# A kernel's first loads: half of x asked for later, half behind the first weight block, and 13 warm-up matmuls in place of 18

## Chip, cores and metric

The kernel runs on one core of one Trainium2 chip. The metric is the device time of one execution in microseconds (us). The time before is the median of three executions.

## What is computed

For each of 8 batches, an index picks one of 8 weight matrices. The batch's rows x (256 x 1024) are multiplied by it, giving y. y then goes through a 1024 x 1024 projection `W_up` plus the low-rank correction of the one expert (of 4) whose gate logit is largest. x is added at the end.

```python
y = jnp.einsum('bsi,boi->bso', x, weight[adapter_ids])
logits = y_flat @ gate_w.T + expert_bias
one_hot = jax.nn.one_hot(jnp.argmax(logits, axis=-1), E)
base_out = jnp.einsum('bth,oh->bto', y, W_up)
z = jnp.einsum('nh,erh->ner', y_flat, lora_A)
delta = jnp.einsum('neh,ne->nh', jnp.einsum('ner,ehr->neh', z, lora_B), one_hot)
out = x + base_out + delta
```

Everything is float32 in and out.

## The kernel before

**Arithmetic.** To keep float32 accuracy on TensorE (PE), each operand is split in two: a high part, which ScalarE (ACT) makes by casting to the matmul's format (`x_hi`, `first_w_hi`, `w_hi_part`), and a low part, which VectorE (DVE) makes by subtracting the high part from the original (`x_lo`, `first_w_lo`, `w_lo_part`). Each product is then several matmuls. For y it is two for each chunk of 128 inputs: L745 with the high weights on both parts of x (512 columns), and L747 with the low weights on the high part of x (256 columns).

**Staging.** For each batch, `first_product` makes y in 8 blocks of 128 outputs. Block n needs one 512 KB piece of weights, called W0, W1, ... here. Each block is 8 pairs of L745 and L747, one pair for each chunk k. The x of a batch (1 MB) comes in two halves of 512 KB: chunks 0 to 3 are the first half, chunks 4 to 7 the second. ACT and DVE split x in four quarters of two chunks, and W0 in four quarters as well; later weight blocks are split in halves. `block_done` counts finished blocks, and ACT then copies a part of the result (`small`, L361) which DVE adds up (L533). After the 8 blocks come the projection, the gates and the correction, then the next batch.

**Order of the work at the start.** All orders are written out by hand. The queue of SyncE (SP) first reads the batch's matrix index from memory into a register. That takes two loads, both at L212: one of the address of `ids`, one of the index itself. Only then can it issue the DMA of W0 (L221), then W1, W2, W3, and from there pieces of `W_up` (L232) and W4 to W6 in turn. ACT's queue issues the two halves of the first x at once (L453), since they depend on no index. DVE meanwhile clears a tile (L706), casts it (L708), and PE runs `WARM` matmuls on these zeros (L730), whose results nobody uses. PE takes its instructions in order, so the first true matmul can't start before the last of these.

The first true matmul (L745 of block 0, k = 0) waits for the first quarter of x and the first of W0, both split. PE then waits again at k = 2, 4 and 6 for the next quarters of each:

```python
if n == 0 and k % QK == 0:
    pe.wait_ge(w_ready, k // QK + 1)
if c == 0 and k % XK == 0:
    pe.wait_ge(x_ready, b * XQ + k // XK + 1)
```

Of the kernel before, what the change touches and what calls it, by code (L numbers as in the profile page):

```python
# [25 lines left out]
def build(nc, xT, x, ids, w, w_up, gl, lora_b, bias, out):  # L26
    B, S, H = x.shape
    KC = H // P
# [16 lines left out]
    XQ = 4  # L45
    XK = KC // XQ
    XD = 2
    XS = KC // XD
# [2 lines left out]
    PARTS = 7  # L51
    SUMS = 5
    STEPS = 9
    WARM = 18
    BLOCKS = B * OC
    assert T == 2 and 4 * ER == P and HALF == 512 and B >= 4 and 2 * GL <= P

# [18 lines left out]
    with ExitStack() as ctx:  # L76
# [22 lines left out]
        x_raw = nc.alloc_sbuf_tensor_at("x_raw", [P, 2, KC, S], F32, offset=x_at)  # L99
# [39 lines left out]
        def sem(name):  # L139
            return ctx.enter_context(nc.semaphore(name))  # L140

        x_raw_in = [sem(f"x_raw_in{d}") for d in range(XD)]
# [7 lines left out]
        warm_step = sem("warm_step")  # L150
# [59 lines left out]
        def _(sp):  # L210
            def adapter(b):
                i = sp.value_load(ids[0:1, b:b + 1])  # L212
                i = i + (i < 0) * A
                i = i * (i > -1)
                i = i + (i > A - 1) * (A - 1 - i)
                return sp.snap(i, min_val=0, max_val=A - 1)

            def load_w(n, i):
                if n >= RAWS:
                    sp.wait_ge(block_done, n - RAWS + 1)  # L220
                sp.dma_start(w_raw[:, n % RAWS, :], w[bass.ds(i * OC + n % OC, 1), :, :].rearrange("a p n -> (a p) n")  # L221
                             ).then_inc(w_raw_in[n % RAWS], 16)
# [40 lines left out]
            def load_blocks(first, stop, i):  # L263
                for n in range(first, min(stop, BLOCKS)):
                    if n % OC == 0:
                        i = adapter(n // OC)
                    load_w(n, i)
                return i

            i = adapter(0)  # L270
            i = load_blocks(0, 4, i)
            for n in range(4, OC):
                load_unit(n - 4)
                i = load_blocks(n, n + 1, i)
# [6 lines left out]
            i = load_blocks(OC, OC + RAWS - 1, i)  # L281
            load_x(1)
            i = load_blocks(OC + RAWS - 1, OC + RAWS, i)
# [4 lines left out]
            for b in range(1, B):  # L288
# [5 lines left out]
                i = load_blocks(first, first + 3, i)  # L294
                load_rows(b)
                i = load_blocks(first + 3, first + OC - 1, i)
                if b + 1 < B:
                    load_x(b + 1)
                i = load_blocks(first + OC - 1, first + OC, i)
# [29 lines left out]
        def _(act):  # L329
            def x_hi(b, q):  # L330
                act.wait_ge(x_raw_in[q * XD // XQ], (b + 1) * 16)
                ks = slice(q * XK, (q + 1) * XK)
                act.copy(x_hilo[:, 0, ks, :], x_raw[:, 1, ks, :]).then_inc(x_hi_ready, 1)  # L333

            def first_w_hi(q):
                act.wait_ge(w_raw_in[0], 16)
                part = slice(q * QK * P, (q + 1) * QK * P)
                act.copy(w_hi[:, 0, part], w_raw[:, 0, part]).then_inc(w_hi_ready, 1)
# [109 lines left out]
                for n in splits_after(b):  # L448
                    w_hi_part(n)

            for d in range(XD):
                ks = slice(d * XS, (d + 1) * XS)
                act.dma_start(x_raw[:, 1, ks, :], xT[0, :, ks, :]).then_inc(x_raw_in[d], 16)  # L453
            for q in range(XQ - 1):
                x_hi(0, q)
            for q in range(QUARTERS // 2):
                first_w_hi(q)
            x_hi(0, XQ - 1)
            for q in range(QUARTERS // 2, QUARTERS):
                first_w_hi(q)  # L460
            for n in range(1, AHEAD):
                w_hi_part(n)
# [8 lines left out]
        def _(dve):  # L471
            def x_lo(b, q):
                dve.wait_ge(x_hi_ready, b * XQ + q + 1)
                ks = slice(q * XK, (q + 1) * XK)
                dve.tensor_tensor(x_hilo[:, 1, ks, :], x_raw[:, 1, ks, :], x_hilo[:, 0, ks, :].bitcast(F32),  # L475
                                  ALU.subtract).then_inc(x_ready, 1)

            def first_w_lo(q):
                dve.wait_ge(w_hi_ready, q + 1)
                part = slice(q * QK * P, (q + 1) * QK * P)  # L480
                dve.tensor_tensor(w_lo[:, 0, part], w_raw[:, 0, part], w_hi[:, 0, part].bitcast(F32),  # L481
                                  ALU.subtract).then_inc(w_ready, 1)
# [223 lines left out]
            dve.memset(warm_f[:, :], 0.0).then_inc(warm_step, 1)  # L706
            dve.wait_ge(warm_step, 1)
            dve.tensor_copy(warm[:, :], warm_f[:, :]).then_inc(warm_ready, 1)  # L708
            for q in range(XQ - 1):
                x_lo(0, q)  # L710
            for q in range(QUARTERS // 2):
                first_w_lo(q)
            x_lo(0, XQ - 1)
            for q in range(QUARTERS // 2, QUARTERS):
                first_w_lo(q)
            for n in range(1, AHEAD):
                w_lo_part(n)
# [8 lines left out]
        def _(pe):  # L726
            def warm_up():
                pe.wait_ge(warm_ready, 1)
                for _ in range(WARM):
                    pe.matmul(ps_y[0][:, :], warm[:, 0:P], warm[:, :], start=True, stop=True)  # L730
# [177 lines left out]
```

## Time and profile before

| | |
|---|---|
| median of 3 runs | 386.61 us (386.48 to 386.88) |
| the profiled execution, own time | 386.45 us |
| its span, first to last instruction | 384.4 us |
| PE busy | 375.4 us (98%) |
| DVE busy | 263.5 us (69%) |
| ACT busy | 163.0 us (42%) |

All positions below are microseconds from the start of the span. The profiled execution is 2.05 us longer than its span, and 0.16 us below the median. A busy share tells how much an engine worked over the whole span; what the change can move lies in the first 12 us, and must be read there.

### The profile page before, as it was taken

Reading aid. Unit: us, or ns where it says so; the run is one execution under the profiler, and the core shown is the slowest. Engines: PE = TensorE matmul, PEld = TensorE weight load, DVE = VectorE, ACT = ScalarE, POOL = GpSimd, SP = SyncE. Lnnn points to the kernel's source line nnn. Section 1 sums busy time; section 2 is a strip of 40 time slices with the busy share of each in tenths; the row PEclk is TensorE's granted clock in tenths of the full one; section 3 lists DMA queues with packets and bytes.
Section 4 is the critical chain, followed back from the end, with each engine's and each line's share of the span. In section 5 each row is a group of like instructions: output and inputs, shape, how many; then the busy total and the mean of one; then the engine's idle time right before and its main releaser. Section 6 shows DMA issues by size and latency. Waiting matters only on the chain.

```text
span 384.4 us, 5419 instructions
## 1 busy us (share of the span) xinstructions
PE 375.4 (98%) x1946; PEld 317.2 (83%) x1946; DVE 263.5 (69%) x501; ACT 163.0 (42%) x329; POOL 4.7 (1%) x15
## 2 busy tenths in 40 slices
PE   6999999999999999999999999999999999999996
PEld 5888888888888788887888878888888878888885
DVE  4878766787658997579636795477864788446743
ACT  5658524554146623565114642255412554044300
POOL 1000200000000000000000000000000000000000
PEclk9999999999999999999999999999999999999999
DMA  7999946860089600875037640476304861160002
GB/s 240 413 378 353 410 192 220 319 226 2 0 309 333 233 2 14 287 271 195 2 122 247 234 163 2 165 282 202 119 0 175 318 218 59 49 226 0 2 0 109
DMA packets 19081, 68.12 MB, mean 177 GB/s; under 512 B 2288, under 2 KB 2416, under 8 KB 19056
## 3 DMA queue, kind: packets, MB, share of 16 engines
q1 hardware_dynamic: 18768, 66.74, 48.4%
q10 hardware_dynamic: 288, 1.05, 0.8%
q8 instruction: 15, 0.25, 0.3%
q14 instruction: 10, 0.08, 0.1%
HBM read 59.39 MB, written 8.39 MB: 176 GB/s over the span
## 4 chain that ended last, share of the span: by engine, by line
PE 83%; DMA 5%; DVE 3%; issue 3%; ACT 2%; SPq 1%; POOLq 1%; POOL 0%; DVEq 0%
PE ps_y L745 26%; PE ps_y L747 13%; PE ps_u L752 6%; PE ps_u L754 5%; PE ps_u L756 5%; DMA gl_raw<-gl_dram 4%; PE ps_g L765 4%; PE ps_v L752 4%; PE ps_v L756 4%; PE ps_v L754 4%; PE ps_p L752 2%; PE ps_p L754 2%; PE ps_p L756 2%; DVE w_lo L488 2%; ACT w_hi L346 1%
## 5 line engine op out<-in xcount | busy, mean ns | idle before, releaser
L745 PE MATMUL ps_y<-x_hilo,w_hi 128*128 128x512 f32 x512 | 181.0, 398 | 1.4 <-DVE w_lo L481 1.1
L747 PE MATMUL ps_y<-x_hilo,w_lo 128*128 128x256 f32 x512 | 143.7, 281 | 0.0
L745 PEld LDWEIGHTS ps_y<-x_hilo,w_hi 128*128 128x128 f32 x512 | 96.1, 188 | 25.6 <-DVE w_lo L481 1.5
L747 PEld LDWEIGHTS ps_y<-x_hilo,w_lo 128*128 128x128 f32 x512 | 96.7, 189 | 0.3
L488 DVE TENSOR_TENSOR w_lo<-w_raw,w_hi 128x512 fp32r<-128x512 f32 x126 | 81.2, 687 | 16.7 <-ACT w_hi L346 15.7
L361 ACT COPY small<-ps_y 128x256 f32<-128x256 f32 x64 | 23.8, 372 | 116.4 <-PE ps_y L747 116.4
L346 ACT CAST w_hi<-w_raw 128x512 fp32r<-128x512 f32 x126 | 71.8, 623 | 0.7 <-DMA w_raw<-w_dram 0.7
L533 DVE TENSOR_TENSOR y_raw<-ps_y,small 128x256 f32<-128x256 f32 x64 | 27.1, 423 | 52.4 <-ACT small L361 52.3
L752 PE MATMUL ps_u<-up_hi,y_parts 128*128 128x512 f32 x112 | 44.6, 398 | 0.0
L754 PE MATMUL ps_u<-up_lo,y_parts 128*128 128x512 f32 x112 | 43.8, 391 | 0.0
L756 PE MATMUL ps_u<-up_hi,y_parts 128*128 128x512 f32 x112 | 43.7, 390 | 0.0
L364 ACT CAST y_parts<-y_raw 128x512 fp32r<-128x512 f32 x50 | 28.8, 619 | 11.4 <-DVE y_raw L539 11.4
L544 DVE TENSOR_TENSOR y_parts<-y_raw,y_parts 128x512 fp32r<-128x512 f32 x50 | 32.5, 685 | 1.3 <-ACT y_parts L364 0.9
L752 PE MATMUL ps_v<-up_hi,y_parts 128*128 128x512 f32 x64 | 25.9, 404 | 2.3 <-DVE y_parts L544 2.3
L551 DVE TENSOR_TENSOR rows<-ps_u,rows 128x512 f32<-128x512 f32 x26 | 17.9, 687 | 13.9 <-PE ps_u L756 13.9
L756 PE MATMUL ps_v<-up_hi,y_parts 128*128 128x512 f32 x64 | 25.1, 392 | 0.0
L754 PE MATMUL ps_v<-up_lo,y_parts 128*128 128x512 f32 x64 | 25.0, 391 | 0.0
L756 PEld LDWEIGHTS ps_u<-up_hi,y_parts 128*128 128x128 f32 x112 | 21.0, 188 | 4.6
L752 PEld LDWEIGHTS ps_u<-up_hi,y_parts 128*128 128x128 f32 x112 | 21.1, 188 | 4.4 <-DVE up_lo L495 0.2
L754 PEld LDWEIGHTS ps_u<-up_lo,y_parts 128*128 128x128 f32 x112 | 21.0, 188 | 3.8
L475 DVE TENSOR_TENSOR x_hilo<-x_raw,x_hilo 128x512 fp32r<-128x512 f32 x32 | 20.5, 686 | 4.2 <-ACT x_hilo L333 3.5
L378 ACT CAST zT<-ps_y 128x128 fp32r<-128x128 f32 x16 | 3.5, 269 | 41.1 <-PE ps_y L784 41.1
(81 smaller groups left out, 355.5 us busy)
## 6 DMA issues: line engine op xcount, KB each, us to landing
w_raw<-w_dram SPq DMA_DIRECT2D x64, 512.0 KB, 4.4
rows<-x_dram SPq DMA_DIRECT2D x16, 512.0 KB, 5.8
out_dram<-rows SPq DMA_DIRECT2D x15, 512.0 KB, 2.6
x_raw<-xT_dram SPq DMA_DIRECT2D x14, 512.0 KB, 5.0
up_raw<-w_up_dram SPq DMA_DIRECT2D x8, 512.0 KB, 11.6
up_stage<-w_up_dram SPq DMA_DIRECT2D x8, 512.0 KB, 13.9
x_raw<-xT_dram ACTq DMA_DIRECT2D x2, 512.0 KB, 4.3
lb_raw<-lora_b_dram SPq DMA_DIRECT2D x4, 128.0 KB, 13.9
```

What stands on the lines that cost most here:

```text
L346: act.copy(w_hi[:, n % RING, part], w_raw[:, n % RAWS, part]).then_inc(w_hi_ready, QUARTERS // HALVES)
L361: act.copy(small[:, c % 2, :], ps_y[c % 2][:, S:2 * S]).then_inc(y_small_ready, 1)
L364: act.copy(y_parts[:, p, :, 0, :], y_raw[:, p, :, 1, :]).then_inc(y_hi_ready, 1)
L475: dve.tensor_tensor(x_hilo[:, 1, ks, :], x_raw[:, 1, ks, :], x_hilo[:, 0, ks, :].bitcast(F32), ALU.subtract).then_inc(x_ready, 1)
L488: dve.tensor_tensor(w_lo[:, n % RAWS, part], w_raw[:, n % RAWS, part], w_hi[:, n % RING, part].bitcast(F32), ALU.subtract).then_inc(w_read ...
L533: dve.tensor_tensor(y_raw[:, p:p + 2, c % Q, 1, :], ps_y[c % 2][:, 0:S].rearrange("p (t n) -> p t n", t=T), small[:, c % 2, :].rearrange(" ...
L544: dve.tensor_tensor(y_parts[:, p, :, 1, :], y_raw[:, p, :, 1, :], y_parts[:, p, :, 0, :].bitcast(F32), ALU.subtract).then_inc(y_ready, 1)
L745: pe.matmul(ps_y[c % 2][:, :], w_hi[:, n % RING, cols], x_hilo[:, :, k, :], start=(k == 0), stop=False)
L747: last = pe.matmul(ps_y[c % 2][:, S:2 * S], w_lo[:, n % RAWS, cols], x_hilo[:, 0, k, :], start=False, stop=(k == KC - 1))
L752: pe.matmul(ps[:, :], y_parts[:, p, k, 0, :], up_hi[:, q, k, :], start=start, stop=False, skip_group_check=True)
L754: pe.matmul(ps[:, :], y_parts[:, p, k, 0, :], up_lo[:, q, k, :], start=False, stop=False, skip_group_check=True)
L756: return pe.matmul(ps[:, :], y_parts[:, p, k, 1, :], up_hi[:, q, k, :], start=False, stop=stop, skip_group_check=True)
```

## The change

Four edits, all in the start of the first batch:

- the number of matmuls on zeros is 13 instead of 18
- ACT waits for the end of DVE's first memset (`warm_step`) and then issues the DMA of the first half of x only
- SP issues the DMA of the second half of x, right behind that of W0 and ahead of that of W1
- ACT and DVE take the splits in another order: x quarters 0 and 1, W0 quarters 0 and 1, then x quarter 2, W0 quarter 2, x quarter 3, W0 quarter 3. Before it was x quarters 0, 1 and 2, W0 quarters 0 and 1, x quarter 3, W0 quarters 2 and 3

```diff
-    WARM = 18
+    WARM = 13
...
             i = adapter(0)
-            i = load_blocks(0, 4, i)
+            i = load_blocks(0, 1, i)
+            sp.dma_start(x_raw[:, 1, XS:KC, :], xT[0, :, XS:KC, :]).then_inc(x_raw_in[1], 16)
+            i = load_blocks(1, 4, i)
...
-            for d in range(XD):
-                ks = slice(d * XS, (d + 1) * XS)
-                act.dma_start(x_raw[:, 1, ks, :], xT[0, :, ks, :]).then_inc(x_raw_in[d], 16)
-            for q in range(XQ - 1):
+            act.wait_ge(warm_step, 1)
+            act.dma_start(x_raw[:, 1, 0:XS, :], xT[0, :, 0:XS, :]).then_inc(x_raw_in[0], 16)
+            for q in range(XQ // XD):
                 x_hi(0, q)
             for q in range(QUARTERS // 2):
                 first_w_hi(q)
-            x_hi(0, XQ - 1)
             for q in range(QUARTERS // 2, QUARTERS):
+                x_hi(0, q)
                 first_w_hi(q)
...
-            for q in range(XQ - 1):
+            for q in range(XQ // XD):
                 x_lo(0, q)
             for q in range(QUARTERS // 2):
                 first_w_lo(q)
-            x_lo(0, XQ - 1)
             for q in range(QUARTERS // 2, QUARTERS):
+                x_lo(0, q)
                 first_w_lo(q)
```

How the instructions stand on ACT from its first one, before (`x_raw_in0` and `x_raw_in1` count the two halves of x, `w_raw_in0` is W0's arrival):

```order
L453 DMA x_raw_52<-xT_dram 128x1024 x2
L333 ACT_TABLE_LOAD
L333 CAST x_hilo_53<-x_raw_52 128x512 [waits x_raw_in0] x2
L333 CAST x_hilo_53<-x_raw_52 128x512 [waits x_raw_in1]
L338 CAST w_hi_51<-w_raw_49 128x256 [waits w_raw_in0] x2
L333 CAST x_hilo_53<-x_raw_52 128x512 [waits x_raw_in1]
L338 CAST w_hi_51<-w_raw_49 128x256 [waits w_raw_in0] x2
L346 CAST w_hi_51<-w_raw_49 128x512 [waits w_raw_in1]
```

and on ACT of the changed kernel, where the lines stand two or three higher:

```order
L456 DMA x_raw_52<-xT_dram 128x1024 [waits warm_step]
L335 ACT_TABLE_LOAD
L335 CAST x_hilo_53<-x_raw_52 128x512 [waits x_raw_in0] x2
L340 CAST w_hi_51<-w_raw_49 128x256 [waits w_raw_in0] x2
L335 CAST x_hilo_53<-x_raw_52 128x512 [waits x_raw_in1]
L340 CAST w_hi_51<-w_raw_49 128x256 [waits w_raw_in0]
L335 CAST x_hilo_53<-x_raw_52 128x512 [waits x_raw_in1]
L340 CAST w_hi_51<-w_raw_49 128x256 [waits w_raw_in0]
L348 CAST w_hi_51<-w_raw_49 128x512 [waits w_raw_in1]
```

One DMA has left ACT, the other now waits, and both casts of the second half of x stand behind the first two of W0. DVE's subtractions have moved in the same way. On SP, from its first instructions, the piece of the difference is:

```order
 L221 ISA x2
 L221 DMA w_raw_49<-w_dram 128x1024
+L272 DMA x_raw_52<-xT_dram 128x1024
 L221 ISA
 L221 DMA w_raw_49<-w_dram 128x1024
```

The second half of x has come in between W0 and W1; every later DMA of SP's stands one place further back.

## Rows read from the trace of the kernel before

**Rows 1.** The page's engines, and PE's longest wait for a split.

```profile
PE 375.4 (98%) x1946; PEld 317.2 (83%) x1946; DVE 263.5 (69%) x501; ACT 163.0 (42%) x329; POOL 4.7 (1%) x15
...
PE ps_y L745 <- DVE w_lo L481: 1.1, 1, 1.1
```

**Rows 2.** Chain that ended last, 0 to 14 us: start us, us, what.

```profile
0.73 0.86 SPq L212
...
1.62 2.19 SPq L212
...
4.47 3.36 DMA w_raw<-w_dram
...
7.85 0.41 ACT w_hi L338
...
8.77 0.50 PE ps_y L745
...
11.73 0.13 PE ps_y L747
```

**Rows 3.** The index loads: whole run (x8), then the second batch's; ns min/median/max.

```profile
L212 SPq TENSOR_LOAD <-ids_dram_ptr x8: 862/1870/3115, 0.7 to 293.1; - x8
L212 SPq TENSOR_LOAD <-ids_dram x8: 467/551/2186, 1.6 to 295.1; - x8
...
L212 SPq TENSOR_LOAD <-ids_dram x1: 1222/1222/1222, 20.7 to 20.7; - x1
```

**Rows 4.** Timeline, 0 to 9 us: start us, us, engine line operation.

```profile
0.74 0.86 ACTq L453 DMA_DIRECT2D x_raw<-xT_dram  x2
...
0.92 0.48 DVE L706 MEMSET warm_f<- 128x512 f32 x1 [0.92 <-PEq L901]
...
1.92 5.74 PE L730 MATMUL ps_y<-warm 128*128 128x512 f32 x18 [1.92 <-DVE warm L708]
...
4.70 1.83 ACT L333 CAST x_hilo<-x_raw 128x512 fp32r<-128x512 f32 x3 [1.78 <-DMA x_raw<-xT_dram]
5.35 1.90 DVE L475 TENSOR_TENSOR x_hilo<-x_raw,x_hilo 128x512 fp32r<-128x512 f32 x3 [3.48 <-ACT x_hilo L333]
...
8.29 0.76 DVE L481 TENSOR_TENSOR w_lo<-w_raw,w_hi 128x256 fp32r<-128x256 f32 x2 [1.03 <-ACT w_hi L338]
```

**Rows 5.** Tile x_raw, 0 to 14 us: its two DMAs, issue to landing.

```profile
DMA to landing us min/median/max: 3.9/4.3/4.7
```

**Rows 6.** Timeline, 9 to 15.3 us.

```profile
9.89 1.15 ACT L346 CAST w_hi<-w_raw 128x512 fp32r<-128x512 f32 x2 [0.20 <-DMA w_raw<-w_dram]
...
10.62 2.73 DVE L488 TENSOR_TENSOR w_lo<-w_raw,w_hi 128x512 fp32r<-128x512 f32 x4
...
11.00 0.39 PE L745 MATMUL ps_y<-x_hilo,w_hi 128*128 128x512 f32 x1
...
11.34 1.14 ACT L346 CAST w_hi<-w_raw 128x512 fp32r<-128x512 f32 x2 [0.30 <-DMA w_raw<-w_dram]
...
11.69 0.39 PE L745 MATMUL ps_y<-x_hilo,w_hi 128*128 128x512 f32 x1
...
15.20 1.14 ACT L346 CAST w_hi<-w_raw 128x512 fp32r<-128x512 f32 x2 [0.16 <-DMA w_raw<-w_dram]
```

**Rows 7.** Windows of 0.5 us: busy of each engine, granted clock, DMA share, GB/s.

```profile
7.00:7.50 0.50, 0.50 (x3) 0.20 (x2) 0.26 (x1) 0.00 (x0) 0.00 (x0) 1.00 1.05 426
...
9.00:9.50 0.50, 0.50 (x4) 0.40 (x4) 0.43 (x2) 0.50 (x3) 0.00 (x0) 1.00 0.60 156
```

**Rows 8.** Matmuls on zeros, 0 to 5 us, then 5.3 to 8 us.

```profile
L730 PE MATMUL ps_y<-warm x8: 393/628/794, 1.9 to 5.0; 128*128 128x512 f32 x8
...
L730 PE MATMUL ps_y<-warm x11: 388/389/398, 5.0 to 7.3; 128*128 128x512 f32 x11
```

**Rows 9.** Timelines of ACT and POOL, from 30 us.

```profile
31.30 0.37 ACT L361 COPY small<-ps_y 128x256 f32<-128x256 f32 x1 [1.45 <-PE ps_y L747]
...
38.94 2.80 POOL L325 TENSOR_TENSOR gl_parts<-gl_raw,gl_parts 128x432 fp32r<-128x432 f32 x1 [7.01 <-ACT gl_parts L382]
```

## Prediction

> **What bounds the kernel now.** I read the page first. PE is busy for 375.4 of 384.4 us [rows 1], so what happens before PE's first true matmul is nearly all that can be won outside PE's own work, and any shift of the first block moves everything behind it. Next I read the chain that ended last, over its first 12 us, because it says what the first true matmul waited for [rows 2]. SP loads the address of the indices (0.73 to 1.59), then the index (1.62 to 3.81), computes W0's address and issues W0's DMA at 4.47. That lands 3.36 us later, at 7.83. ACT's cast and DVE's subtraction take it to PE's start at 8.77, and block 0 is done at 11.73 + 0.13 = 11.86 (the chain's last piece of it). From here I use "block 0 done" as the mark: 11.86 before.
>
> Then the timeline of the same stretch [rows 4]. The first half of x is asked for at 0.74 and ACT starts on it at 4.70, after 3.96 us. Three of its four casts run from 4.70 to 6.53 without a pause, so the second half of x was there by 5.92. The times to landing agree: 3.9 us for the first half; 4.7 us for the second, which was issued some 0.43 us after the first, hence about 1.17 + 4.7 = 5.87 [rows 4, 5]. So x is early by 2 us, and W0 is late. The matmuls on zeros end at 1.92 + 5.74 = 7.66, another 1.1 us before PE's start, and PE's wait row says so too [rows 1, 4].
>
> **Later memset, one DMA alone.** The odd row in the chain is the index load: 2.19 us [rows 2]. The same load takes a median of 0.55 us and at least 0.47 in the eight batches, and 1.22 in the second one. The load of the address takes 0.86 at the start, when nothing moves, and a median of 1.87 in the run, where transfers are mostly in flight [rows 3]. In the first batch the index load runs beside the start of x's transfers, which were asked for at 0.74. The change asks for x when the memset ends, 0.92 + 0.48 = 1.40; with the hand-over I take 1.45, later by 0.71. If x's bytes are that much later too, an index load of the quiet kind, 1.62 + 0.86 = 2.48, is over as they begin. I take 0.86, the one load of the trace that ran in silence; the bounds are 0.47 and the full 2.19. W0's issue then moves from 4.47 by 2.19 - 0.86 = 1.33 to 3.14.
>
> The Trainium skill, "DMA: Bandwidth & Descriptors", section "Latency and other measured facts", says the memory's latency is about 0.2 us on average but 2 us at high load. By that rule the shortening is real and the sum stays as it is; the spread between 0.47 and 3.1 us in the rows agrees with it [rows 3].
>
> **When W0 lands.** Two bounds. By itself W0 needs 3.36 us from issue: 3.14 + 3.36 = 6.50. But it comes behind the first half of x, and two transfers of 512 KB that start from silence landed 5.87 - 0.74 = 5.13 us after the first was asked for [rows 4, 5]: 1.45 + 5.13 = 6.58. The later one holds: 6.58, against 7.83. The first half of x lands at 1.45 + 3.96 = 5.41. Its two casts end at about 6.6 and its two subtractions at about 7.4 (each pair at the pace of 0.61 us, the first subtraction 0.65 us behind the first cast, as in rows 4). W0's first subtraction begins at about 7.3 and PE starts 0.48 us after that begins (8.29 to 8.77): near 7.8.
>
> **When the second half of x lands.** It now follows W0 on SP's queue. One transfer of 512 KB takes 1.29 us in the steady stream: W2 landed at about 11.32, W4 at about 15.18, with W3 and one piece of W_up between, so three transfers in 3.86 us [rows 6]. 6.58 + 1.29 = 7.87; before it was 5.87. This is the price of the change: what was idle-time work on ACT and DVE is now on the path. Behind a landing at L: cast of x quarter 2, its subtraction 0.65 later, W0 quarter 2 another 0.61 later, x quarter 3 another 0.36 (0.34 is the pace of the small subtractions [rows 4], and the cast of quarter 3 must be done), W0 quarter 3 another 0.61: it begins at L + 2.23. PE starts on k = 6 0.48 later, L + 2.71. Before, k = 6 started at 11.00 and the block was done at 11.86 [rows 2, 6], so done is L + 2.71 + 0.86 = L + 3.57 = 11.44. The direct way, PE's start at 7.8 + 3.09 (8.77 to 11.86), would be 10.9, so the second half of x decides, with short waits of PE at k = 4 and k = 6. Net: 11.44 - 11.86 = **-0.42 us**.
>
> **W1.** It too moves back one place on SP's queue, but up by W0's 1.25 us. It lands 1.29 behind the second half of x, at 9.16, or, if the hole in the stream that stands there now is kept (W1 was at 9.87, 2.04 behind W0, with 156 GB/s at 9.00:9.50 against 426 in the stream [rows 6, 7]), at 9.91. From landing to PE: the subtraction starts 10.62 - 9.87 = 0.75 behind, and takes 0.69 (2.73 us for four, overlapped by some hundredths, [rows 6]): 9.91 + 1.48 = 11.39 for block 1's first matmul, which stood at 11.69. So this path gives -0.30 at the latest. I take **-0.4 us** between the two. Block 2's and block 3's weights come when they came before (the stream carries the same bytes and starts 0.7 later, but has no gap between x and W0), and are needed 5 us after they land from W3 on.
>
> **The 13 matmuls.** Five fewer. Late in the stretch they are 0.23 us apart, (7.3 - 5.0) / 10 [rows 8], so the last ends near 7.66 - 1.15 = 6.5. With 18 they would end at 7.66, just under PE's new start of 7.8: this edit is worth nothing as long as the second half of x decides. It costs nothing unless the clock falls (below).
>
> **What is behind.** No later wait takes the gain back: POOL's subtraction at 38.94, which PE's gates wait for, is released by ACT, and ACT has worked without a pause since 31.30, when PE's block 7 released it [rows 9]; all of that moves with PE. Sum: 386.61 - 0.4 = **386.2 us**; the profiled one 386.45 would be 386.05, with a span of 384.0.
>
> **Rivals.**
> 1. The second half of x comes late in its new place. If the hole of 0.75 us falls on it and not on W1, it lands at 8.62 and block 0 is done at 12.19: +0.33, 386.9. The hole follows W0 in the profile, which speaks for it; that it may belong to W1's or W2's bytes speaks against.
> 2. The index load doesn't get shorter; it was slow because it was the first. W0 is issued at 4.47 and lands at 7.83 as now, the second half of x at 9.12, block 0 is done at 12.69: **+0.83 us, 387.4, slower**. It decides from the point where L + 3.57 passes 11.86: L = 8.29, W0 at 7.00, thus W0's issue at 3.64 and an index load of 1.36 us. For it: no load of the index happened in silence. Against it: the address load, just as cold, took 0.86.
> 3. The load is halfway, 1.22 as in the second batch [rows 3]: issue 3.50, W0 at 6.86, x at 8.15, done 11.72: -0.14, 386.5. The Trainium skill, "Runtime: NRT & Kernel Launch", section "The ~15µs preamble/postamble breakdown", gives 1.3 us for such a load as one trip to memory, without regard to traffic; that would nearly be this case, but the 0.47 and 0.86 of the rows speak against a fixed price.
> 4. More than forecast. One transfer alone may ramp faster than two did: W0 needed 2.3 us from where x's bytes stopped (about 5.5) to its landing. If x's first half ramps likewise and W0 follows without a gap, W0 lands near 6.2 and the second half of x at 7.5: -0.8, 385.8. PE's start bounds it at 10.9 - 11.86 = -1.0.
> 5. PE's clock. The matmuls on zeros took 628 ns at first and 389 from 5.0 us on, with starts 0.43 and 0.23 us apart [rows 8]: the lower level (1.2 GHz) until PE had worked for some 3 us, the upper one (2.4 GHz) after it, although the profile's clock column reads 1.00 throughout. The idle time ahead of PE's start grows from 1.1 to 1.3 us, with two short waits behind it. Should the clock fall, 3 us of work at half rate cost +1.5: 387.7. The 1.1 us before did not bring it down, so I give this little.
>
> **How the numbers follow.** Chances: the forecast 0.37, case 3 0.11, case 1 0.12, case 2 0.14, case 4 0.22, case 5 0.04. Faster or slower by 0.2% is 0.77 us, about what a measurement of this kernel can tell. Some three quarters of case 4 and a little of the forecast are faster by that much: 0.20. Cases 2 and 5, not quite all, are slower: 0.16. The same: 0.64. The range reaches from case 4 (385.7) to case 2 (387.4), widened a little for what I may have left out: 385.6 to 387.5.
>
> **What would show it.** In the changed kernel's chain the second L212 piece should be near 0.9 us and W0's DMA should start near 3.1 and land near 6.6. PE's first true matmul should stand near 7.8, with a wait of about 0.4 us ahead of k = 4 and 0.3 ahead of k = 6, and block 0 done near 11.4. PE's matmuls behind block 1 should be the same, all shifted. The prediction is wrong if the index load stays at 2 us, if the second half of x lands after 8.3, or if later waits of PE are new.

## Result and the profile after

The changed kernel takes 388.75 us (median of 20 runs, 387.45 to 391.68), the kernel before 386.65 (20 runs, 386.17 to 387.20): ratio 1.0054, 95% interval 1.0039 to 1.0068. It is slower by 2.1 us, where 0.4 us faster was forecast. The changed kernel's runs also spread over 4 us, those of before over 1.

The profiled execution took 387.59 us, with a span of 385.7, so it is one of the faster ones: 1.3 us more than the span before. Its chain that ended last, from the start (start us, us, what), answers to [rows 2]:

```profile
0.73 0.85 SPq L212
...
1.61 0.46 SPq L212
...
2.74 0.39 SPq L221
...
3.18 6.26 DMA x_raw<-xT_dram
...
9.46 0.63 ACT x_hilo L335
...
10.11 0.69 DVE x_hilo L478
...
11.20 0.50 PE ps_y L748
...
12.98 0.13 PE ps_y L750
```

The index load fell from 2.19 to 0.46 us, and W0's DMA starts at 2.74 instead of 4.47. But the chain no longer runs through W0. It runs through the second half of x, asked for at 3.18 and landed 6.26 us later, at 9.44. Block 0 is done at 12.98 + 0.13 = 13.11; before it was 11.86. These +1.25 us are the whole difference of the two spans. The timeline of the same stretch answers to [rows 4]:

```profile
1.44 0.38 ACTq L456 DMA_DIRECT2D x_raw<-xT_dram  x1
...
1.92 5.05 PE L733 MATMUL ps_y<-warm 128*128 128x512 f32 x13 [1.92 <-DVE warm L711]
...
5.22 1.14 ACT L335 CAST x_hilo<-x_raw 128x512 fp32r<-128x512 f32 x2 [2.09 <-DMA x_raw<-xT_dram]
...
7.34 0.71 ACT L340 CAST w_hi<-w_raw 128x256 fp32r<-128x256 f32 x2 [0.98 <-DMA w_raw<-w_dram]
...
8.26 0.50 PE L748 MATMUL ps_y<-x_hilo,w_hi 128*128 128x512 f32 x1 [1.28 <-DVE w_lo L484]
...
9.46 0.62 ACT L335 CAST x_hilo<-x_raw 128x512 fp32r<-128x512 f32 x1 [1.41 <-DMA x_raw<-xT_dram]
...
11.20 0.50 PE L748 MATMUL ps_y<-x_hilo,w_hi 128*128 128x512 f32 x1 [1.26 <-DVE w_lo L484]
```

W0 landed at 7.32, 4.58 us after its issue against 3.36 before. PE starts at 8.26, half a microsecond earlier than before, works for four chunks and then waits 1.26 us. The second half of x came 2.12 us behind W0, not 1.29. PE's waits over the whole run answer to the row of waits in [rows 1]:

```profile
PE ps_y L748 <- DVE w_lo L484: 2.5, 2, 1.3
PE ps_v L755 <- DVE y_parts L547: 2.3, 4, 0.6
```

One wait of 1.1 us has become two that sum to 2.5; the rest is as it was. The stream of bytes is where the time went; windows of 0.5 us (the last two numbers are the share of the DMA engines and GB/s):

```profile
4.50:5.00 0.50, 0.50 (x2) 0.39 (x2) 0.00 (x0) 0.00 (x0) 0.00 (x0) 1.00 0.60 139
...
6.00:6.50 0.50, 0.50 (x4) 0.41 (x3) 0.50 (x2) 0.36 (x1) 0.00 (x0) 1.00 1.05 418
...
7.00:7.50 0.50, 0.00 (x0) 0.00 (x0) 0.17 (x1) 0.16 (x1) 0.00 (x0) 1.00 0.90 221
7.50:8.00 0.50, 0.00 (x0) 0.00 (x0) 0.22 (x1) 0.50 (x2) 0.00 (x0) 1.00 1.02 287
```

There are two holes, one between the first half of x and W0, one while the second half of x is under way; in the second the engines are busy (0.90 and 1.02) but move only 221 to 287 GB/s. The kernel before had its own hole, behind W0 [rows 7], but nothing that PE needed stood in it.

Each load counts sixteen completions on its semaphore, and has landed with the last. For the second half of x the trace has the first of them at 7.72, the twelfth at 8.80 and the last at 9.44: some parts of the load come long after the others.

### The profile page after: what moved, and what is told of

It reads as the page before. It is cut to its first block, busy times and chain, and to the rows that moved or that the text cites. A ratio compares the mean times of both kernels' runs of the same rounds, so it can differ in the third digit from the quotient of the medians.

```text
span 385.7 us, 5409 instructions
## 1 busy us (share of the span) xinstructions
PE 375.2 (97%) x1941; PEld 316.3 (82%) x1941; DVE 263.3 (68%) x501; ACT 162.8 (42%) x329; POOL 4.7 (1%) x15
## 3 DMA queue, kind: packets, MB, share of 16 engines
HBM read 59.39 MB, written 8.39 MB: 176 GB/s over the span
## 4 chain that ended last, share of the span: by engine, by line
PE 83%; DMA 6%; DVE 3%; issue 3%; ACT 2%; SPq 1%; POOLq 1%; POOL 0%; DVEq 0%
PE ps_y L748 26%; PE ps_y L750 13%; PE ps_u L755 6%; PE ps_u L757 5%; PE ps_u L759 5%; DMA gl_raw<-gl_dram 4%; PE ps_g L768 4%; PE ps_v L755 4%; PE ps_v L759 4%; PE ps_v L757 3%; PE ps_p L755 2%; PE ps_p L757 2%; PE ps_p L759 2%; DMA x_raw<-xT_dram 2%; DVE w_lo L491 1%
```

## Experiments

Each kernel was timed beside the kernel before on the same chip: the median of before was 386.60 us beside experiments 1 to 4, 386.49 beside 5 to 8 and 386.56 beside 9 to 15. With each run comes its span and its mean granted clock. "Low clock" below means a mean of 0.996 or less; none of the 94 runs of the kernel before beside these experiments was below 0.998.

**1. The late asking alone.**

```diff
+            act.wait_ge(warm_step, 1)
             for d in range(XD):
                 ks = slice(d * XS, (d + 1) * XS)
                 act.dma_start(x_raw[:, 1, ks, :], xT[0, :, ks, :]).then_inc(x_raw_in[d], 16)
```

> The kernel before with one edit: ACT waits for the first memset and then asks for both halves of x, as before in this order; 18 matmuls on zeros, old order of splits. Theory A (the place of the second half of x behind W0 is what costs): the index load is near 0.5 us here too and W0's DMA starts near 2.75, but W0 comes behind 1 MB of x, so it lands at 7.3 to 7.6 against 7.83 before; the second half of x lands near 6.6 and delays nobody; block 0 is done near 11.5, 0.2 to 0.5 us earlier than before, and the time is 386.2 to 386.5 with no run far off. Rival B (asking for x later is itself the loss): block 0 done after 12.5, 387.5 or more.

387.03 us (12 runs, 386.58 to 387.39), ratio 1.0004 (0.9994 to 1.0015): at best nothing, and 0.4 us more by the medians. No run's clock was below 0.999. The timeline of its ACT:

```profile
5.35 1.14 ACT L333 CAST x_hilo<-x_raw 128x512 fp32r<-128x512 f32 x2 [1.74 <-DMA x_raw<-xT_dram]
7.18 0.62 ACT L333 CAST x_hilo<-x_raw 128x512 fp32r<-128x512 f32 x1 [0.69 <-DMA x_raw<-xT_dram]
8.47 0.71 ACT L338 CAST w_hi<-w_raw 128x256 fp32r<-128x256 f32 x2 [0.67 <-DMA w_raw<-w_dram]
```

W0 was issued at 2.73, 1.7 us earlier than before, and yet landed at 8.45, 0.6 us later. The index load had not been what W0 waited for in the end: 1 MB of x is ahead of it, asked for 0.7 us later. Neither theory had this: A had W0 at 7.3 to 7.6 and a time of 386.2 to 386.5. Block 0 was done at 12.52, where B had "after 12.5", but the time is under B's 387.5. The second half of x, too, landed later than two loads from silence had: 7.16 is 5.72 us after the asking, against 5.13.

**2. 18 matmuls on zeros in the changed kernel.** The edit is `WARM = 18`.

> The changed kernel with 18 matmuls on zeros instead of 13. Theory C (PE stands idle for longer ahead of its first true matmul, and in some runs the granted clock is then at the lower level for a stretch, which makes the changed kernel's runs spread from 387.4 to 391.7): with 18 the runs lie within about 0.7 us of each other, at 387.4 to 387.9, which is the profiled 1.25 us of the late second half of x and nothing else. Rival D (the spread comes from the loads, whose landing differs from run to run): the median stays near 388.7 and runs still reach 390.

388.68 us (11 runs, 387.87 to 390.48), ratio 1.0055 (1.0037 to 1.0072). That is what rival D forecast. C had 387.4 to 387.9. Only one run of 11 has a low clock (0.996, and it is the longest), but runs at 1.0 reach 389.79, so something else than the clock spreads the time too.

**3. 13 matmuls on zeros in the kernel before.** The edit is `WARM = 13`.

> The kernel before with 13 matmuls on zeros instead of 18 and nothing else. Theory C: idle time ahead of the first true matmul grows from 1.1 to about 2.2 us; some runs are 1.5 to 3 us longer and show a mean clock of 0.996 or below, the median is 0.3 to 2 us above that of the kernel before. Rival D: 386.6 and no spread, since no load has moved.

386.59 us (12 runs), ratio 1.0003 (0.9989 to 1.0018). Nine runs at 386.19 to 386.63 with a clock of 0.999 or 1.0, three at 387.77, 388.12 and 388.24, all with 0.996. Fewer matmuls on zeros don't move the median (C had it at least 0.3 us up), but in a quarter of the runs they cost 1.6 us (388.12 against 386.53, the medians of the two groups), and the clock is what those runs have in common.

**4. The second half of x on ACT's queue.**

```diff
             act.dma_start(x_raw[:, 1, 0:XS, :], xT[0, :, 0:XS, :]).then_inc(x_raw_in[0], 16)
+            act.dma_start(x_raw[:, 1, XS:KC, :], xT[0, :, XS:KC, :]).then_inc(x_raw_in[1], 16)
...
-            sp.dma_start(x_raw[:, 1, XS:KC, :], xT[0, :, XS:KC, :]).then_inc(x_raw_in[1], 16)
```

> The changed kernel with the second half of x on ACT's queue right behind the first, still after the memset; 13 matmuls on zeros and the new order of splits. Theory A: the second half lands near 6.6, W0 at 7.3 to 7.6, block 0 is done near 11.5 in the profile, so the fastest runs are 386.0 to 386.4, 1.3 us below the fastest of the changed kernel; by theory C some runs are still long. Rival B: fastest runs at 387.4 as in the changed kernel.

388.47 us (7 runs, 387.02 to 389.11), ratio 1.0039 (1.0019 to 1.0060). The one run with its clock at 1.0 took 387.02; the other six, 388.26 to 389.11, had 0.994 to 0.996. Theory A's 386.0 to 386.4 for the fastest was missed: W0 landed at 8.33, late as in experiment 1. The profile is of a run with a low clock, and shows what happens. Its windows (PE busy first, the granted clock third from the end):

```profile
6.30:9.60 3.30, 1.10 (x5) 0.63 (x4) 1.77 (x4) 1.45 (x5) 0.00 (x0) 0.98 1.03 410
9.80:13.10 3.30, 3.30 (x13) 2.84 (x12) 3.30 (x7) 3.00 (x7) 0.00 (x0) 0.54 1.03 417
13.20:16.50 3.30, 3.30 (x21) 2.89 (x21) 2.51 (x5) 1.41 (x3) 0.00 (x0) 1.00 1.03 417
```

and its matmuls in block 0 (ns min/median/max):

```profile
L748 PE MATMUL ps_y<-x_hilo,w_hi x5: 628/628/663, 9.3 to 11.9; 128*128 128x512 f32 x5
```

The zeros ended at 1.92 + 5.15 = 7.07, PE idled 2.2 us until 9.27, and then the granted clock fell from the upper level (2.4 GHz) to the lower one (1.2 GHz) for most of the second window, whose mean is 0.54, while PE worked through block 0. The matmuls took 628 ns instead of 391. The Trainium skill, "TensorE: Matmul & The Clock Gate", section "HAM oscillation — how this bites in real kernels", says that waits for DMA between groups of matmuls let the clock drop, so that the next group starts at the lower rate; this trace agrees, and experiment 9's profile has such a wait without a fall.

**5. The same with 18 matmuls on zeros.** Experiment 4's kernel with `WARM = 18`.

> The changed kernel with the second half of x on ACT's queue behind the first (no DMA of x behind W0) and 18 matmuls on zeros: what is left of the change is the later asking and the new order of splits. Theory C2 (a load that comes later takes its time from block 0, and beside that an idle time of PE of 2 us or more, where the zeros end early, lets the clock fall in many runs): no run with a mean clock below 0.998, and 387.0 as with the old order of splits, 386.6 to 387.4. Rival E (the new order of splits is a cost of its own): 387.5 or more with the clock at 1.0.

387.60 us (7 runs, 387.15 to 387.72), ratio 1.0027 (1.0016 to 1.0038), and no run below 0.999. Against experiment 4 the falls are gone, and 0.9 us with them. The expected 387.0 was missed, and the time is in rival E's range: beside experiment 1, which differs only by the order of splits, it is 0.6 us longer (+1.1 and +0.4, each beside its own runs of before). In the profiles block 0 was done at 12.86 here and 12.52 there. Of these 0.34 us, 0.13 are W0's landing (8.58 against 8.45) and about 0.2 a short wait at k = 6 that the new order brings; the rest of the 0.6 has no cause on record.

**6. The place behind W0 without the late asking.** The changed kernel without `act.wait_ge(warm_step, 1)`, with `WARM = 18`.

> The changed kernel without ACT's wait and with 18 matmuls on zeros: the first half of x is asked for at 0.74 as in the kernel before, the second stands behind W0. Theory A (the place behind W0 costs, the asking time little): x's first half lands near 4.4, the index load is between 0.5 and 2.2 us; W0 lands at 6.8 to 7.8 and the second half of x 1.3 to 2.1 later, so block 0 is done at 12.2 to 13.0 and the time is 387.0 to 387.8. Rival B (the late asking is the main loss): 386.7 or less.

388.01 us (6 runs, 387.64 to 389.98; two at 0.996, despite 18 matmuls on zeros), ratio 1.0056 (1.0037 to 1.0075); 387.0 to 387.8 was expected. The four at a full clock have a median of 387.82. The index load took 1.38 us, W0 was issued at 3.64 and landed at 6.88; the second half of x landed at 9.44, 2.56 us behind it. The place, together with the new order of splits, costs as much as the whole change.

**7. The changed kernel again.**

> The changed kernel itself once more, for a second profile and the mean clock of each run beside kernels on the same chip. Expected: median near 388.7, fastest near 387.5; the runs with a mean clock of 0.996 or less are on average 1.5 us above those at 0.999 or 1.0. Rival: clock and time of a run have nothing to do with each other.

387.81 us (8 runs), ratio 1.0056 (1.0031 to 1.0080), where 388.7 was expected: two medians of the same kernel differ by 0.9 us. Six runs at 387.48 to 387.92 (0.999 or 1.0), two at 390.83 and 390.85 (0.990, 0.991). With the 20 runs of the result: 9 of 28 have a clock of 0.996 or less, with a median of 390.25; the 19 others have a median of 387.83 and reach 389.27. The nine are of two kinds: five at 0.996 with a median of 389.45, 1.6 us above the 19, and four at 0.990 or 0.991 with 390.84, 3.0 above. The profile, of a run at a full clock, gives W0 at 6.89 and the second half of x at 9.70.

**8. W0 in two DMAs** (kernel before; `w_half_in` is a new semaphore, and the first two quarters wait for it).

```diff
+                src = w[bass.ds(i * OC + n % OC, 1), :, :].rearrange("a p n -> (a p) n")
+                if n == 0:
+                    sp.dma_start(w_raw[:, 0, 0:HK * P], src[:, 0:HK * P]).then_inc(w_half_in, 16)
+                    sp.dma_start(w_raw[:, 0, HK * P:KC * P], src[:, HK * P:KC * P]).then_inc(w_raw_in[0], 16)
+                    return
...
-                act.wait_ge(w_raw_in[0], 16)
+                act.wait_ge(w_half_in if q < QUARTERS // 2 else w_raw_in[0], 16)
```

> The kernel before with the DMA of W0 cut in two DMAs of 256 KB with a semaphore each, so that the first two quarters can be split while the second half of W0 is under way. Nothing else changed. If PE's start hangs on the last byte of W0, its first half lands about 0.6 us earlier (7.2), PE starts near 8.1 to 8.2 after zeros that end at 7.7, W1's landing (9.9, plus 1.48) then bounds block 1 at 11.4 against 11.69: 386.3, 0.3 us less. Rival: the transfer's fixed part and one more DMA issue (0.4 us) on SP take it back: 386.6 or more.

387.29 us (11 runs), ratio 1.0025 (1.0016 to 1.0033): the rival's side, though not by its reason. PE did start at 8.13, 0.64 us earlier, but ACT then waited 1.8 us for W1 and PE 1.2 us for block 1. W1 landed at 10.78, 2.48 us behind the second half of W0: again a transfer that stands early in the queue came late.

**9. More matmuls on zeros in PE's idle times** (the changed kernel, `WARM = 16`).

```diff
                     for k in range(KC):
+                        if n == 0 and k == HK:
+                            for _ in range(5):
+                                pe.matmul(ps_l[:, :], warm[:, 0:P], warm[:, :], start=True, stop=True)
```

> The changed kernel with its two idle times of PE filled: 16 matmuls on zeros ahead (13 in the changed kernel), and five more on zeros, into a bank that nothing reads, between chunks 3 and 4 of block 0, where PE waits about 1.3 us for the second half of x. The loads are untouched. Theory C2 (the falls of the clock come from idle time ahead of and inside block 0): no run below a mean clock of 0.998; the runs lie between 387.4 and 388.4, median near 387.8, as the fast ones of the changed kernel. Rival D (the long runs come from late loads): as many runs over 389 as before (10 of 28 had 389 or more).

388.47 us (5 runs, 387.33 to 389.01), ratio 1.0038 (1.0025 to 1.0051), every clock at 1.0, as C2 says, but with the median 0.7 us above C2's 387.8. Five runs are few: if each had the changed kernel's chance of a low clock (9 in 28), a set of five would still show none about one time in seven. The spread without a low clock is D's share. The profile is of the longest run. Its chain, and PE's waits for W0 and x:

```profile
3.33 7.53 DMA x_raw<-xT_dram
...
10.88 0.63 ACT x_hilo L335
...
14.40 0.13 PE ps_y L753
...
PE ps_y L751 <- DVE w_lo L484: 2.6, 2, 2.4
```

The second half of x landed at 10.86, 1.42 us later than in the changed kernel's first profile; block 0 was done at 14.53, 1.42 later, and the span is 387.0 against 385.7. Most of this was W0's: twelve of its sixteen completions were there at 6.59, but the last came at 8.64, 1.32 us later than in the first profile. So the idle time ahead of PE's first true matmul was not filled here. It was 2.4 us, more than in experiment 4, and yet the clock stayed at 1.0. The experiment doesn't show that filling cures the falls.

**10. Eight matmuls on zeros in the kernel before.** `WARM = 8`.

> The kernel before with 8 matmuls on zeros instead of 18: PE is then idle for some 3 us ahead of its first true matmul. Theory C2: most runs show a mean clock of 0.996 or less, or a clock that rises only after the first blocks, and are 1.3 to 3 us above the kernel before: median 388 to 389.5. Rival: as with 13, where 9 of 12 runs were at 386.6, the median does not move.

388.23 us (6 runs, 387.64 to 389.16), ratio 1.0049 (1.0036 to 1.0062): every run is long. Windows of its profile:

```profile
5.50:8.80 3.30, 0.33 (x2) 0.32 (x2) 2.42 (x5) 2.10 (x6) 0.00 (x0) 0.97 0.98 333
8.90:12.20 3.30, 3.30 (x12) 2.78 (x12) 2.49 (x5) 2.22 (x6) 0.00 (x0) 0.53 0.94 349
```

PE idles for 3.0 us, then block 0 runs at the lower level. With no load moved, this gives the price of too few matmuls on zeros: +1.7 us by the medians, and +1.1 to +1.6 for the three runs at 0.996. The three others are longer, at 388.3 to 389.2, with a mean clock of 0.999. Perhaps the clock rose late there, before the stretch over which the mean is taken; no profile of such a run was made.

**11. SP held until the second half of x has landed** (the changed kernel, `WARM = 18`).

```diff
             sp.dma_start(x_raw[:, 1, XS:KC, :], xT[0, :, XS:KC, :]).then_inc(x_raw_in[1], 16)
+            sp.wait_ge(x_raw_in[1], 16)
             i = load_blocks(1, 4, i)
```

> The changed kernel with 18 matmuls on zeros, where SP issues W1 and all that follows only when the second half of x has landed. Theory F (the second half of x lands 2.1 to 2.8 us behind W0 instead of 1.3 because W1 and the next already draw on the same 16 engines): it lands about 1.3 us behind W0, at 8.2 to 8.5, block 0 is done at 11.8 to 12.1, and then PE waits for W1, which is issued near 8.3 and lands near 11.5: the whole is no faster. Theory G (whatever is second on SP's queue at that time lands late, alone or not): the second half of x still lands at 9.4 or later.

389.20 us (5 runs, two of them with a low clock), ratio 1.0073 (1.0060 to 1.0086), as W1 now comes late: PE waits 1.8 us for it, and in the profile, of a run at 0.996, the clock falls right behind that wait. But the second half of x, issued at 3.18 as in the changed kernel, landed at 8.31 instead of 9.44, 1.26 us behind W0 (7.05).

**12. The order of splits alone.** The kernel before with the two loops on ACT and DVE as in the change.

> The kernel before with the new order of splits and nothing else: the third quarter of x, which is there before W0, is now split after two quarters of W0. Expected: PE starts at 8.77 as before, but on DVE one more subtraction of 0.69 us stands behind W0's landing, so that PE waits for k = 4 or k = 6: block 0 is done 0.2 to 0.4 us later, 386.8 to 387.0. Rival: the order costs nothing, 386.5, and the 0.6 us between the two kernels with both halves of x on ACT's queue (387.6 and 387.0) come from elsewhere.

386.75 us (11 runs), ratio 1.0004 (0.9995 to 1.0012). Not to be told from nothing by the times. In the profile W0 landed at 7.81 as before (7.83), and block 0 was done at 12.09, 0.2 us later, as expected: PE is late by that at k = 6.

**13 to 15. Why the transfer behind W0 is late.** In the kernel before, SP waits for W0 ahead of W2; the same with W0 in two DMAs; and in the changed kernel with `WARM = 18`, SP waits for W0 ahead of W1:

```diff
-            i = load_blocks(0, 4, i)
+            i = load_blocks(0, 2, i)
+            sp.wait_ge(w_raw_in[0], 16)
+            i = load_blocks(2, 4, i)
```

```diff
             sp.dma_start(x_raw[:, 1, XS:KC, :], xT[0, :, XS:KC, :]).then_inc(x_raw_in[1], 16)
+            sp.wait_ge(w_raw_in[0], 16)
             i = load_blocks(1, 4, i)
```

> The kernel before, where SP issues W2 and all that follows only when W0 has landed. Theory F (transfers queued further back draw on the same engines, and the one behind W0 lands late): W1 lands at 9.2 instead of 9.9, which nobody waits for; W2 is issued near 7.9 and lands at 11.3 to 11.8, and the time stays at 386.5 to 387.0. Theory G (the lateness has nothing to do with what is queued behind): W1 lands at 9.9 or later.

386.64 us (11 runs), ratio 1.0000 (0.9991 to 1.0009). W0 landed at 7.56; ACT's casts of W1 start at 9.33 without a wait, against 9.89 with one before. That is theory F's forecast, but it doesn't show F, since experiment 3, with the loads of the kernel before and no hold, has much the same. Its ACT, then this one's:

```profile
9.52 1.14 ACT L346 CAST w_hi<-w_raw 128x512 fp32r<-128x512 f32 x2
...
9.33 1.14 ACT L348 CAST w_hi<-w_raw 128x512 fp32r<-128x512 f32 x2
```

W1 landed 1.44 us behind W0 there and 1.43 here. In experiments 3 and 10 it was W2 that came late, 2.4 us behind W1. So in the kernel before the hole falls on W1 in some executions and on W2 in others, and either way PE doesn't wait.

> The kernel before with W0 in two DMAs of 256 KB, and SP issues W2 and all that follows only when both have landed. Theory F: PE starts near 8.2 as with the two halves alone, W1 lands near 9.2 and no more holds block 1 up (it waited 1.2 us without the hold): block 1 starts at 11.1 to 11.3 against 11.69 before, 386.0 to 386.3, faster than both kernels. Theory G: 387.3, as with the halves alone.

387.10 us (11 runs), ratio 1.0013 (1.0004 to 1.0022). F's forecast of 386.0 to 386.3 was missed, and G's 387.3 is nearer. The profile is of the longest run (388.52). PE starts at 8.39, but W1, with nothing issued behind it until 8.24, landed at 10.08, 2.0 us behind the second half of W0, where F had 9.2. This speaks against F as a full account. W2's casts, issued late, start at 13.65 after 2.3 us of waiting; ACT's copy of block 0's result stands behind them, and PE waits 1.4 us for it.

> The changed kernel with 18 matmuls on zeros, where SP issues W1 and all that follows only when W0 has landed. Theory F: W0 lands near 6.9, the second half of x 1.3 us later near 8.2, block 0 is done near 11.9 as in the kernel before; W1 is issued near 7.0, lands near 10.4, and holds block 1 up by some tenths: 386.5 to 387.3, 1.2 us or more below the same kernel without the hold (388.68). Theory G: the second half of x lands at 9.4, 388 or more.

387.56 us (11 runs, 386.93 to 388.21), ratio 1.0027 (1.0018 to 1.0036), 1.1 us below the same kernel without the hold (experiment 2). Seven of its 11 runs are below the shortest there, 387.87. Timeline of its ACT:

```profile
6.68 0.71 ACT L341 CAST w_hi<-w_raw 128x256 fp32r<-128x256 f32 x2 [0.24 <-DMA w_raw<-w_dram]
...
7.92 0.62 ACT L336 CAST x_hilo<-x_raw 128x512 fp32r<-128x512 f32 x1 [0.53 <-DMA x_raw<-xT_dram]
```

W0 at 6.66 and the second half of x at 7.90, 1.24 us behind it. With nothing issued behind them before W0 has landed, these two land where the prediction had them (6.58 and 7.87), and the sixteen completions of the second half of x lie between 7.40 and 7.90 instead of 7.72 and 9.44. Block 0 was done at 11.57, 0.29 us earlier than in the kernel before; 0.42 was forecast. The gain is lost again later: PE waits 0.1 us for W1, W2's casts start at 12.22 instead of 11.34 [rows 6], the copy of block 0's result stands behind them on ACT (13.27), and PE waits 0.3 us for it. In this profile the blocks behind it are slower too (last section). So the hold trades one late load for another.

No kernel tried beats the kernel before.

## Why the prediction was wrong, step by step

**Index load: right, and stronger.** 0.86 us was taken, 0.46 came, in all nine profiles with the late asking; with one half of x asked for early it took 1.38 (experiment 6). W0 was issued at 2.74; 3.14 was forecast. The Trainium skill's "DMA: Bandwidth & Descriptors", section "Latency and other measured facts", has memory latency rise under load by a large factor, and the trace agrees: 0.46 us in silence, 2.19 beside x's transfers. The same section's floor of about 600 ns for such a load is not confirmed: 0.46.

**When W0 lands: the first step that failed.** The sum took 5.13 us for two transfers from silence, as the two halves of x had needed, and got 6.58. It was 7.32, and 6.89 to 8.64 in the other profiles of the changed kernel's loads (experiments 2, 7, 9). With the transfers behind held back it was 6.66 and 7.05 (experiments 15 and 11). So the sum is near the earliest that was seen, and left out that the same load's landing differs by up to 1.75 us from one execution to the next. The holding back may help W0; two profiles don't show it, since 6.89 without it is below 7.05 with it.

**When the second half of x lands: the step that decided.** The term of the sum that failed is the 1.29 us behind W0, the pace of the steady stream. 2.12, 2.81, 2.10, 2.56 and 2.22 came (the result, experiments 7, 2, 6 and 9). The place behind W0 thus put the second half of x at 9.44 to 10.86 instead of 7.87. This is rival 1, whose price of 0.75 us for the hole was near (0.83 in the result), and its side, that the hole stays behind W0 whatever the transfer there carries, was the right one. Experiments 11 and 15 show that the place alone doesn't do it: with the issue of W1 held back the interval was 1.26 and 1.24. What is issued behind the load, while it is under way, matters here. By which path it does, and how many transfers it takes, was not tested, and in experiment 14 the hold didn't help W1. The kernel before already paid the hole on W1 [rows 6] or on W2 without PE waiting for them, which is why it was harmless there.

**From landing to done: right.** L + 3.57 gives 9.44 + 3.57 = 13.01; measured 13.11. In experiment 9: 14.43 and 14.53. Of PE's two forecast waits, 0.4 us at k = 4 and 0.3 at k = 6, the first was 1.26 and the second 0.2.

**W1 and what is behind: right.** No later wait of PE is new; 1.25 us at block 0 are 1.3 us of span.

**The 13 matmuls: half right.** By the medians their worth is nothing, as said (experiments 2 and 3). But rival 5, the clock, was given 0.04 and a price of 1.5 us, and a low clock came in 9 of 28 runs of the changed kernel; the longest run of the kernel before in any comparison took 388.60, at 0.998. The price was right: 1.6 us in experiment 3, 1.5 in experiment 4 (388.5, the median of the six, against the one at 387.02) and 1.6 for the changed kernel's runs at 0.996. The 3.0 us of those at 0.990 and 0.991 is twice that and fits two stretches at the lower level; no such run was profiled. What failed is the chance. PE's idle time ahead of its start was taken as 1.3 us and is 1.28 in the profile, but 1.26 inside block 0 come to it, since the second half of x is late. How much of the 9 in 28 the five matmuls themselves brought isn't shown: with 18 and the second half of x behind W0 (experiments 2 and 6), 3 runs of 17 had a low clock, and these numbers are too small to tell the two shares apart.

**The sum.** Late loads are the 1.2 us between 386.6 and the 387.8 of the runs with a full clock. The result's median of 388.75 holds more: seven of its 20 runs have a low clock, and four with a full one are above 388.5. Without the seven the median is 387.86. But experiment 2, with one low clock in 11, has 388.68, and experiment 7, the changed kernel again, 387.81, so how the last 0.9 us divides between the clock and still later loads stays open. The parts do not add up neatly: the place behind W0 with the new order gives +1.5 (experiment 6; +1.3 for its runs with a full clock), late asking alone +0.4 at most, the order 0.2. The point of decision was right: L = 8.29, which rival 2 names, was passed, though not by its mechanism.

**Two slips of the working.** W0's first subtraction is let begin at 7.3 while DVE still works on x until 7.4, and rival 4's 385.8 enters the range as 385.7. Neither bears on what went wrong.

## What to carry to other kernels

A transfer that is moved to a place behind another is not priced by the pace of the steady stream: read in the trace how much later than its neighbour the one now standing there lands, and what is issued behind it while it is under way. Read it in several executions, since the late place moves. Freeing the address of a load early gives nothing when the bytes ahead of it are asked for later in exchange. And where a change makes PE wait in two places instead of one, time it in many runs: a fall of the clock shows in some executions only, and a single profile can miss it.

## What was not expected of the hardware

- The clock fell after 2.2 us without a matmul in experiment 4's profile (a mean of 0.54 over 9.80 to 13.10), and its mean was low in six of the seven runs; with the same 13 matmuls on zeros ahead of a PE start at 8.69 only in three of twelve (experiment 3). It fell after 1.8 us in experiment 11's profile, and not after 2.4 us in experiment 9's. The gap differs from run to run, because the matmuls on zeros end earlier or later with the instant at which the clock rises: at 7.80 in experiment 3's profile, 0.9 us ahead of PE's start. In experiment 5, where they ended at 8.33 and PE started at 9.52, no run of seven fell. How the gap and the fall hang together in each run stays open.
- The pace of the first batch's blocks takes one of two values without an edit that would explain it. Five blocks, from the start of one ACT copy to that of the fifth after it, took 31.30 - 17.44 = 13.86 us in the kernel before and in the changed one (32.55 - 18.68 = 13.87), but 14.13 in experiments 1 (32.31 - 18.18) and 15 (31.89 - 17.76). Of the 17 profiles ten have the first value and seven the second (experiments 1, 2, 3, 5, 10, 14 and 15), nothing between. From the start of block 1 to the end of the span this is some 0.35 us (373.0 in experiment 1 against 372.7 in the kernel before), nearly the effect that was forecast. What decides it stays open.
- A load of 512 KB lands late by its last parts. Of W0's sixteen completions twelve came between 6.18 and 6.59 in experiment 9 and the last at 8.64; in experiment 15 all sixteen lie between 6.12 and 6.66.
